# Attention kernel on one core: the row maxima's transposition moved beside the outputs' one and into their bank, their split moved to a half-unit's first step, final norms scaled by ScalarE

## The reference, cut to what matters

```python
x = _layernorm(x + L0_attn(x))   # gated state-space block
x = _layernorm(x + L0_ffn(x))    # top-1 of 8 experts
x = _layernorm(x + L1_attn(x))   # 16 heads of 8, scores over all 512 tokens
x = _layernorm(x + L1_ffn(x))    # graph of 6 attention nodes, then a norm of its own
```

```python
scores = jnp.einsum('bqhd,bkhd->bhqk', qh, kh) / jnp.sqrt(dh)
attn = jax.nn.softmax(scores, axis=-1)
ctx = jnp.einsum('bhqk,bkhd->bqhd', attn, vh).reshape(B, S, d)
return ctx @ wo
...
return (x - mu) * jax.lax.rsqrt(var + LN_EPS) * g + b   # at the end of L1_ffn
```

## Time and profile before

| | us |
|---|---|
| runs (3), median | 2198.59 |
| lowest, highest | 2197.19, 2199.01 |
| profiled execution | 2196.76 |
| its span, first to last instruction | 2195.0 |
| PE busy | 2023.1 (92%) |
| DVE busy | 1725.2 (79%) |
| ACT busy | 1487.4 (68%) |
| POOL busy | 315.0 (14%) |

### The profile page before, as it was taken

One profiled execution on the slowest core, in us unless ns is written; L12 is line 12 of the kernel. 1 busy time (PEld: TensorE's weight loads), 2 busy tenths in 40 slices (PEclk: granted clock), 3 DMA queues, 4 the chain that ended last, 5 costly groups with the idle time before them and its releaser, 6 DMA issues.

```text
span 2195.0 us, 32025 instructions
## 1 busy us (share of the span) xinstructions
PE 2023.1 (92%) x10812; PEld 840.8 (38%) x10812; DVE 1725.2 (79%) x3483; ACT 1487.4 (68%) x2004; POOL 315.0 (14%) x370
## 2 busy tenths in 40 slices
PE   5748887999999999999999999999999999999995
PEld 2224443333333333444444444444444444443331
DVE  5855887788888878887777787788777788878884
ACT  3743552666666677777777777777777777776664
POOL 1100211000000011111111111111111111113213
PEclk9976886999999999999999999999999999999998
DMA  3001224233333366566666656656655566665530
GB/s 104 19 24 48 93 83 110 49 74 71 73 74 74 81 113 114 110 110 110 110 110 110 110 109 109 110 104 111 101 110 105 107 109 108 110 108 100 95 58 25
DMA packets 137899, 200.25 MB, mean 91 GB/s; under 512 B 20290, under 2 KB 55770, under 8 KB 137178
## 3 DMA queue, kind: packets, MB, share of 16 engines
q1 hardware_dynamic: 137742, 198.25, 46.7%
HBM read 75.45 MB, written 23.73 MB: 45 GB/s over the span
## 4 chain that ended last, share of the span: by engine, by line
PE 81%; DVE 12%; issue 4%; ACT 1%; DMA 1%; POOL 0%; DVEq 0%; POOLq 0%; SPq 0%; ACTq 0%
PE bank_s L1052 27%; PE bank_o L1102 22%; PE bank_x L1087 6%; DVE nm L1431 4%; PE bank_m L1115 3%; PE bank_x L1038 3%; PE bank_x L1017 3%; PE bank_x L1025 2%; PE bank_m L1135 2%; PE bank_x L1004 2%; PE bank_x L1161 2%; PE bank_s L955 2%; PE bank_m L1125 1%; PE bank_m L1074 1%; DVE big L1312 1%
## 5 line engine op out<-in xcount | busy, mean ns | idle before, releaser
L1431 DVE TENSOR_REDUCE nm<-bank_s 128x1 f32<-128x512 f32 x2012 | 1311.7, 684 | 335.2 <-PE bank_s L1052 334.1
L842 ACT ACTIVATE big<-bank_x 128x1024 f32<-128x1024 f32 x1024 | 1048.6, 1025 | 479.2 <-PE bank_x L1087 452.1
L1052 PE MATMUL bank_s<-kst,qst 62*128 62x512 f32 x2012 | 813.1, 463 | 41.2 <-DVE nm L1431 37.8
L1087 PE MATMUL bank_x<-qst,kst 64*128 64x512 f32 x2048 | 749.3, 447 | 1.6 <-ACT big L842 1.6
L1052 PEld LDWEIGHTS bank_s<-kst,qst 62*128 62x128 f32 x2012 | 348.8, 185 | 666.1 <-DVE nm L1431 580.9
L1102 PE MATMUL bank_o<-big,at 128*32 128x512 f32 x4096 | 554.7, 614 | 2.2 <-ACT big L842 2.0
L1087 PEld LDWEIGHTS bank_x<-qst,kst 64*128 64x128 f32 x2048 | 304.0, 186 | 10.5 <-issue 6.0
L626 POOL CAST at<-at 128x512 fp32r<-128x512 f32 x112 | 68.3, 610 | 1265.5 <-ACT at L773 1035.5
L628 POOL TENSOR_TENSOR at<-at 128x512 fp32r<-128x512 f32 x112 | 143.5, 1281 | 10.0
L1102 PEld LDWEIGHTS bank_o<-big,at 128*32 128x32 f32 x4096 | 81.1, 108 | 152.6 <-issue 148.6
L850 ACT ACTIVATE big<-bank_x,big 128x128 f32<-128x128 f32 x256 | 68.9, 377 | 28.0 <-DVE big L1468 15.8
(11 more groups left out here) (160 smaller groups left out, 1524.3 us busy)
## 6 DMA issues: line engine op xcount, KB each, us to landing
at<-nodes_d SPq DMA_DIRECT2D x144, 256.0 KB, 5.8
kst<-at SPq DMA_DIRECT2D x288, 128.0 KB
qst<-at SPq DMA_DIRECT2D x288, 128.0 KB
nodes_d<-big SPq DMA_DIRECT2D x48, 256.0 KB, 3.0
at<-w_d SPq DMA_DIRECT2D x48, 193.0 KB, 5.9
at<-x2T_d SPq DMA_DIRECT2D x32, 256.0 KB, 4.6
kst<-at SPq DMA_DIRECT2D x128, 64.0 KB
qst<-at SPq DMA_DIRECT2D x128, 64.0 KB
```

Source lines behind the costliest of these rows:

```text
L842: act.activation(PT[:, kp, h, :, :], ring.take()[0].rearrange("p (c n) -> p c n", c=2), ACT.Exp, scale=x.c.scale).then_inc(S["c_ex"], 1)
L1052: pe.matmul(bank_s[:, n % 2, :], qst[rows, x.r, h, t * P:(t + 1) * P], kst[rows, x.r, h, :], start=True, stop=True).then_inc(S["c_s_ps"], 1)
L1087: mm = pe.matmul(sec(to, j), kst[rows, x.r, h, kc_ * P:(kc_ + 1) * P], qst[rows, x.r, h, :], start=True, stop=True)
L1431: dve.tensor_reduce(nm[:, k, at_n:at_n + 1], bank_s[:, n % 2, :], AX.X, ALU.max, negate=True).then_inc(S["c_red"], 1)
```

## The change

Four things are changed.

1. `maxima` moves from step 1 to step 3, in front of `turn`. It writes bank_o, which is free between `ev_pv` and the next `output`, in place of bank_m; `ev_m` moves behind exp 3, and `output` now also waits for it.
2. `parts` moves from step 6, where it read the group that had just been finished, to step 0 of the half-unit in which this group is transposed. Its first instruction stands behind the step's first reduction, its second behind the second one. Before the loop the split of group 1 is gone, and `maxima` of group 0 waits for bank_o's last reader of the stage before.
3. The final norms are cut up and moved one unit later: VectorE's statistics come one tile at a time between reductions, both normalisations are done by ScalarE as scale * x + shift in steps (0,1) to (0,4), two tiles each, and VectorE computes shift = -mean * rstd (128x4) at (0,0). GpSimd's order within a unit changes with it, and `store_out` comes a unit later, behind `rows_m`.
4. Behind the last unit: the norms of the two units before it stay on VectorE, and the last batch takes `final_gain`, which does GpSimd's product and sum on VectorE.

```diff
@@ PE
-                misc(S["c_mT_ev"], G + 1)
-                pe.transpose(bank_m[0:32, 0:P], mp[:, 0:32], ident[:, :]).then_inc(S["c_mT_ps"], 1)
+                need(pe, S["c_pv_ev"], G - 1)
+                pe.transpose(bank_o[0:32, 0:P], mp[:, 0:32], ident[:, :]).then_inc(S["c_mT_ps"], 1)
...
                     if kp == 0:
                         need(pe, S["c_pv_ev"], G)
+                        need(pe, S["c_mT_ev"], min(G + 2, 2 * (UC + NODES * NB)))
...
-                        if i == 1:
+                        if i == 3:
                             maxima(*led_group(c, q, r, k))
-                        if i == 3:
                             turn(*((last, 1) if k == 0 else (x, 0)))
@@ ACT
+            def final_scale(x, which, tiles):
+                ...
+                need(act, S[f"f_shift{which}"], j + 1)
+                to, of, r_ = ((zn, nT, rs), (x3s, zn, rs2))[which]
+                for t in tiles:
+                    i = act.activation(to[:, cols], of[:, cols], ACT.Identity, bias=shift[which][:, t:t + 1], scale=r_[:, t:t + 1])
...
                         exp(x, k, i)
+                        if (k, i) in ((0, 1), (0, 2)):
+                            final_scale(at_(c, q, r - 3), 1, (2 * i - 2, 2 * i - 1))
+                        if (k, i) in ((0, 3), (0, 4)):
+                            final_scale(at_(c, q, r - 2), 0, (2 * i - 6, 2 * i - 5))
...
-                        if i == 1:
+                        if i == 3:
                             ev_m(*led_group(c, q, r, k))
@@ POOL
             def body(c, q, r):
                 residual_rstd(at_(c, q, r - 1))
-                final_sum(at_(c, q, r - 1))
+                final_sum(at_(c, q, r - 2))
+                final_rstd2(at_(c, q, r - 2))
+                final_rstd(at_(c, q, r - 1))
                 split(at_(c, q, r + 3))
-                final_rstd(at_(c, q, r - 1))
@@ DVE
+FIRST_NORM_AT = [(1, 3, 0), (1, 3, 1), (1, 5, 0), (1, 5, 1), (1, 6, 1)]
+SECOND_STATS_AT = [(1, 1, 0), (1, 1, 1), (1, 2, 0), (1, 2, 1), (1, 6, 0)]
...
+            def final_shift(x, which):
+                ...
+                dve.scalar_tensor_tensor(shift[which], mean[:, :, 0], -1.0, r_, ALU.mult, ALU.mult).then_inc(S[f"f_shift{which}"], 1)
+            def final_gain(x):
+                ...
+                    dve.scalar_tensor_tensor(zn[:, cols], nT[:, cols], mv[:, t, 0:1], lngb[:, 0, :], ALU.subtract, ALU.mult)
+                ...
+                    i = dve.scalar_tensor_tensor(zn[:, cols], zn[:, cols], rs[:, t:t + 1], x2s[:, cols], ALU.mult, ALU.add)
...
-                            if i == 6:
-                                parts(*read_group(c, q, r, k), j)
+                            if i == 0:
+                                parts(*led_group(c, q, r, k), j)
+                            if at_step in FIRST_NORM_AT:
+                                final_norm(last, FIRST_NORM_AT.index(at_step))
+                            if at_step in SECOND_STATS_AT:
+                                final_norm(at_(c, q, r - 2), 2 * (NT + 1) + SECOND_STATS_AT.index(at_step))
+                            if at_step == (0, 0, 0):
+                                final_shift(at_(c, q, r - 2), 0)
+                            if at_step == (0, 0, 1):
+                                final_shift(at_(c, q, r - 3), 1)
```

More of the change, by code:

```diff
@@ L139, in build @@
         x3s = cut2(L)
+        shift = [sb(f"shift{k}", [P, NT])[:, :] for k in range(2)]
         nm = sb("nm", [P, 2, 16])
@@ L1597, in final_norm @@
                     return
-                if step == 0:
+                part, t = step // (NT + 1), step % (NT + 1)
+                cols = slice(t * D, (t + 1) * D)
+                if part == 0 and t < NT:
                     need(dve, S["f_tT_ev"], j + 1)
-                    stats(nT, stt, mv, S["f_link"], NT * j, S["f_mv"])
-                if step == 1:
+                    dve.bn_stats(stt[:, t, :], nT[:, cols]).then_inc(S["f_link"], 1)
+                if part == 0 and t == NT:
+                    need(dve, S["f_link"], NT * (j + 1))
+                    for t in range(NT):
+                        i = dve.bn_aggr(mv[:, t, :], stt[:, t, :])
+                    i.then_inc(S["f_mv"], 1)
@@ L1608, in final_norm @@
-                if step == 3:
+                    dve.bn_stats(stt2[:, t, :], zn[:, cols]).then_inc(S["f_link2"], 1)
+                if part == 2 and t == NT:
+                    need(dve, S["f_link2"], NT * (j + 1))
+                    for t in range(NT):
+                        i = dve.bn_aggr(mv2[:, t, :], stt2[:, t, :])
+                    i.then_inc(S["f_mv2"], 1)
+                if part == 3 and t < NT:
                     need(dve, S["f_rs2"], j + 1)
                     need(dve, S["f_out"], 16 * j)
-                    normalise(x3s, zn, mv2, rs2, S["f_y"])
+                    i = dve.tensor_scalar(x3s[:, cols], zn[:, cols], mv2[:, t, 0:1], rs2[:, t:t + 1], ALU.subtract, ALU.mult)
+                    if t == NT - 1:
+                        i.then_inc(S["f_y"], 1)
```

87 lines of the change are left out of this document (59 added, 28 removed).

## The result

| | before | after |
|---|---|---|
| median of 10 runs each, us | 2199.43 | 2207.30 |
| lowest, highest | 2197.13, 2204.40 | 2202.75, 2210.02 |
| profiled execution, its span | 2196.76, 2195.0 | 2202.75, 2200.6 |

The ratio is 1.0032, interval [1.0022, 1.0042]: slower by 0.2 to 0.4%. The forecast was 2190.8, its range ended at 2207, and it gave "slower" a chance of 0.19. It was wrong in the direction.

The account below looks back on a forecast made before the run. TensorE was taken to set the nodes' pace, with something holding it up in the first attention. Terms: -10 + 10 up to the last node, -7.8 after, giving 2190.8 us; range 2174 to 2207.

Parts of the forecast that it names:

- first attention: First 16 units: transposition and split moves together save 0.31 us per half, 32 halves, -10 us.
- nodes: 40 node units before the last node: the moved split meets GpSimd at (0,0), +0.25 us a unit, +10 us.
- last node: Units 58 to 61: lighter VectorE norms against blocked splits and ScalarE's scalings, -0.45 us a unit, -2 for four.
- units 61 to 63: No unit ahead: half 1's gain less ScalarE's 1.1 gives -2.5; the clock fall of 2100 to 2120 goes, -2.
- drain: After the last unit: shorter final norms -2.6, last division later by 1.3, net -1.3 us.
- hole of step 4: Half 0: TensorE's wait in step 4, into which the 0.22 us transposition moved to step 3 partly falls.
- what the division gives back: Half 0, step 4: reciprocal and division give most of the gain back; of 0.22 + 0.06 us 0.13 is kept.
- meeting at (0,0): Nodes, half 0, step 0: GpSimd's K and Q split blocks the moved cast and subtraction; value products 0.24 us later.
- keeps nothing: Half 1: node_out and the split between reductions of (1,0) and (1,1) make (1,2) wait, cancelling the 0.22 us.
- rival "slower": Meetings cost a node unit 0.6 us, TensorE idles and the clock falls in the last node: +14, 2212 us; chance 0.18.
- moves by the same 3.4 us: SP's queue behind the later rows' DMA: its loads are used a half-unit or more later.
- paid in full: Step 3: the maxima copy has 0.1 us of cover; anything more on ScalarE before it costs its whole time.

Follow-up runs that it names:

- transposition alone: The kernel before with only point 1 of the change (transposition at step 3, bank_o, later copy); 2180.57 us, ratio 0.9918.
- split back at step 6: The changed kernel with the maxima's split put back to step 6; 2185.03 us, ratio 0.9933 to before.
- old norms: The changed kernel with the final norms, GpSimd's order and the end as before (points 3 and 4 undone); 2201.12 us, ratio 1.0009 to before.
- copy first: The changed kernel with ScalarE's copy of the maxima ahead of the scaling at step 3; 2200.01 us, ratio 1.0008 to before.
- first combined kernel: The changed kernel with maxima copy before scaling, x3's store before the rows' loads, split at step 0 up to unit 13, mostly step 6 after; 2176.42 us, 0.9887.
- half 0's split at step 2: The changed kernel with half 0's maxima split at step 2 instead of 0, half 1's still at step 0; 2189.69 us, ratio 0.9956 to before.

## Why the prediction was wrong

The terms of the prediction's sum beside what the ruler shows (us):

| | forecast | measured |
|---|---|---|
| first attention | -10 | -11.2 |
| nodes, and the passage to them | +10 | +15.2, +4.1 |
| last node | -2 | -2.3 |
| units 61 to 63 | -2.5 - 2 | -2.8, +8.7 |
| drain | -1.3 | -3.0 |
| sum | -7.8 | +8.7 |

The sum is off by 16.5 us: 10.4 of units 61 to 63, 9.3 of the nodes and the passage, less 3.2 of the other three. Without the error of units 61 to 63 the sum would be -1.7, without that of nodes and passage -0.6. Either one alone leaves about no change, and only both together make the kernel slower. So two steps failed. One, the larger, is the price of ScalarE's scalings in front of the copy in unit 63: 1.1 us with the clock at full was forecast, and the stretch became 8.7 longer. The other is the price of the nodes, too small, with a queue of SyncE that was called free.

**First attention: right in its sum, not in its parts.** -11.2 measured, -10 forecast. A plain half loses 0.27 us (13.20 to 12.93); 0.31 was forecast. The transposition gives 0.19 of it (13.01 with it alone) and the split 0.08, half of what I had given it. Over the whole stretch the split gives nothing: 439.3 with the transposition alone, 439.8 with the split back at step 6, 439.7 in after. In three of the last halves of this stretch GpSimd already splits K and Q for nodes, and the moved split meets it: 14.15, 15.68 and 14.23 us in after, 13.78, 14.85 and 13.76 with the transposition alone. I had written that GpSimd's split is away from step 0 here. The rest of the -11.2 is that before has six halves that are 1.0 to 1.6 us longer than their like (14.77 for 13.20), and after three, beside one that is long in both. These are the halves in which the clock fell: their granted clock is 0.88 or 0.89, that of their like 1.00. One of them in before, and one of its like:

```profile
519.38:534.15 14.77, 14.04 (x73) 4.96 (x72) 10.67 (x21) 9.54 (x11) 0.00 (x0) 0.88 0.48 125
577.13:590.33 13.20, 12.48 (x73) 4.71 (x72) 10.66 (x21) 9.54 (x11) 0.00 (x0) 1.00 0.54 142
```

I had forecast none of this, so that the sum came out near -10 partly by luck.

**Nodes: the right mechanism, too small.** Forecast +0.25 a unit, measured +15.2 over 39 units, 0.39 each, in three pieces that were each off:
- The transposition gives -0.23 (27.70 to 27.47), where I kept 0.13. I had argued with the hole of step 4 and with what the division gives back. But it does not only move, it nearly disappears: 0.06 us in front of `turn` instead of 0.22. And half B, for which I kept nothing, gives 0.10.
- The meeting at (0,0) costs half A 0.46 (13.87 to 14.33), where I had 0.38. The mechanism was right to the instruction: +0.22 for the cast (forecast +0.23), 0.84 for the subtraction (forecast 0.81). The Trainium skill's rule (SBUF — State Buffer, "Who interferes with whom"), by which the second of two such instructions is fully blocked, is what these rows show.
- Half B loses 0.18 by the split at (1,0), with no meeting. I had written that half 1 "keeps nothing" of the gain, because node_out and the split stand together there; so I had it at 0, and it came out 0.08 longer than before (0.18 less 0.10). That the split costs this is shown by its return to step 6. That node_out beside it is the reason is argued, and no run parts the two.

Together -0.23 + 0.46 + 0.18 = +0.41 by single halves, +0.39 by the whole stretch. Half A and half B are each 0.08 longer than forecast. My rival "slower" had its turning point at 0.45 a unit. The nodes did not reach it; the losses below did the rest.

**SyncE's queue: the step that failed silently.** I wrote that the queue "moves by the same 3.4 us, and what it loads is used a half-unit or more later". I had looked at the loads and not at the stores. A store too holds something: the buffer that VectorE writes next. It costs 2.0 us once, at the first nodes, where the clock stays at 1.00, and 3.5 with the transposition alone, where the clock falls behind it. With the store moved the wait is gone, and with it both. In after the half before the wait is longer as well, 15.82 us with the split at (0,0) and 14.99 with it at step 2: a meeting like those of the nodes.

**Last node: right in its sum by luck, wrong inside.** -2.3 for four units where -2 was forecast, 30.42 a unit where 30.4 was. The old norms with the moved split do as well (-2.8), so that the term was earned by the split's leaving step 6 and not by the norms. The forecast also holds a slip: it sets the 14.21 of the earlier trace rows against 14.00, and its like in the nodes is 13.70. With that the working gives -0.76 a unit and not -0.45. And a pair of scalings costs 0.77 us, not 0.54: one is 0.39, the upper bound that I had named and not used. The nearest row by tile (0.27) read PSUM, the scaling reads SBUF. And moving the copy ahead of them, which I had called "paid in full" and not followed up, gives 0.69 a unit.

**Units 61 to 63: the step with the largest error.** The clock fall at unit 61 is gone in after, as forecast (18.23 us at a granted 0.81 in before, 14.56 at 1.00), and the stretch gained 2.8 (forecast 4.5). It is gone with the old norms too (14.76 at 1.00), and with the copy first a smaller one is there again (15.46 at 0.89), so that the lighter norms are not shown to be its cause. In unit 63 I had priced ScalarE's 1.1 us and a clock at full. There TensorE has no projections for units ahead, so a half took 11.6 and 13.4 us in before and ScalarE is its bound: three pairs in a row, then the copy. The wait is 0.5 us with the old norms, 1.29 with the copy in front and 2.05 behind, and the last is seen in three profiles: after and both kernels that move only its split. Half B takes 21.5, 22.1 and 21.3 us in them, at a granted 0.53 to 0.55 over the 18 us behind the wait. I had this in the rival "slower" (ScalarE's activations in a row make TensorE idle at (0,4), and the clock falls), but in units 58 to 61, where the halves are 15 us long and hide it. It was the right mechanism in the wrong unit.

**Drain: right in sign.** -3.0 where -1.3 was forecast. From the end of the last aggregate to the second statistics it takes 2.6 us (2191.43 to 2194.02) where it took 6.2 (2182.05 to 2188.22): -3.6, since the product with gamma needs no rstd and runs beside it, which the -2.6 left out. The division starts 0.5 later behind the last `turn`, not 1.3.

What stays open is when the clock falls. Behind the wait of 2.05 us it fell far in all three profiles. Behind the one of 1.29 it stayed at 1.00 in two, and in the first combined kernel it was 0.50 from 2129 to 2131 us and the half took 16.1. With half 0's split at step 2 the stretch from (0,3) of unit 63 to the last `turn` took 36.0 us where after took 31.5. That is the clock too: 0.51 still in its last 14.7 us, where after has 0.90 in its last 9.95.

## What to carry to other kernels

Before an instruction of VectorE is moved to an "idle" place, look at what GpSimd does there, and at the neighbours on VectorE too: here the meeting with GpSimd cost 0.46 us a unit, and the place beside node_out 0.18, by a way that isn't shown. When a copy on which a queue waits becomes later, walk the whole queue, its stores included, and ask for each buffer who writes it next. A place must be judged in each stage apart: the same split at step 0 gains 0.7 us a unit in the last node, gives nothing over the first attention, and loses 0.64 a unit in the nodes between. And when a stretch is compared by one profile of each kernel, read the granted clock of both first: six halves at 0.88 in before and three in after are part of what looks like a gain.

## What the runs showed of the hardware

- A small fp32 transposition (32 columns out, 128 in) right in front of four others adds 0.06 us; between other products it had taken 0.22. The next one starts 0.12 after it. Whether this comes of the identity that both stream isn't shown.
- A ScalarE activation of 128x128, SBUF to SBUF, with a scale and a bias for each partition takes 0.39 us from start to start (0.77 a pair).
- Behind one wait of TensorE of 2.05 us the granted clock was 0.53 to 0.55 over 18 us in three profiles, which cost some 6.6 us beyond the wait. Behind a wait of 1.29 us in the same place it was 1.00 in two profiles, and 0.89 over the half in a third.
- A half of the first attention in which the granted clock is 0.88 takes 1.0 to 1.6 us more than its like at 1.00.
